# Fused tokenizer, attention and mixture-of-experts layer: weights of five groups in the rows, one class scatter, the seventh shared chunk behind the expert loop

## The chip, the cores and the metric

One core of one Trainium2 chip runs the whole layer in one launch. The metric is the device time in microseconds (us); lower is better. The engines are TensorE (PE), VectorE (DVE), ScalarE (ACT), GpSimd (POOL) and SyncE (SP). Each has an instruction queue of its own, and they meet in semaphores.

## The reference

For 16 images of 224 x 224 and 16 texts of 128 rows:

```
h = concat(class_token, patches(x) @ W.T + b) * pos      # 65 tokens per image
h = concat(h, txt)                                       # 193 tokens, 128 features
h = h + attention(layernorm(h))   # linear attention with rope, plus a 3-tap filter
x2 = layernorm(h)
shared = (silu(x2 @ sw1) * (x2 @ sw3)) @ sw2             # hidden size 256
scores = x2 @ gate_w.T            # 8 experts; the best 2 of scores + biases
p = sigmoid(two best scores); p = p / sum(p)
y_e = (silu(x2 @ w1[e]) * (x2 @ w3[e])) @ w2[e]
h = h + sum over the two experts of p * y_e + shared
```

## The kernel before, in words

There are 3088 tokens. Two images make a *group*, so there are G = 8 groups, 0 to 7; a group has three tiles of 128 tokens. The 16 class tokens are a 25th tile (`CLS`), handled with group 7. `hrow` holds all tokens as rows.

*Groups.* A loop takes the groups through tokenizing, attention, the second normalization (into `xd`), the gate's scores, the choice of experts (`choices`, line 1006) and the row numbers in the sorted buffer `xs_dram` (`place` on PE, then `places` and `positions` on DVE). Each token stands there twice, once for each of its experts. POOL writes the rows by indirect scatters (line 858), one for each tile and choice; the class tile takes two of 16 rows. So 50 scatters go out in the order of POOL's queue. Beside its features each row carries where its result belongs and a weight. For groups below `EARLIER` = 6, POOL works out both (`goals` and `shares`, lines 826 to 844, with one reciprocal on DVE and one exponential on ACT, `chances`), and `positions` waits for POOL there. For the later groups (tiles from `FROM` = 18) the rows carry weight 1, and the true weight is multiplied in at the end. The last groups are written out by hand on every engine (from lines 1185 on DVE and 1594 on PE).

*Shared FFN.* It goes in chunks of 384 tokens, 0 to 7, and chunk 8 with the class tokens. For each chunk and each half m of the hidden size: `shared_up` (two pairs of products on PE, lines 1574 and 1577), `shared_silu` on ACT (line 676), `shared_mul` on DVE (line 1159); then `shared_down` (PE, line 1589) and `shared_add` (DVE, line 1165). Chunks 0 to 6 have their ups and products ahead of the expert loop, between the last groups' work; chunk 6's down products, and chunks 7 and 8, stand behind it.

*Expert loop.* SP writes padding rows behind each expert's rows (line 411), waits for all scatters and gathers 128-row tiles from `xs_dram` (lines 418 and 435). For 56 tiles PE transposes (line 1660), multiplies by the two up matrices (line 1671, in three terms, for which `round_w13` on ACT and `remainder_w13` on DVE, line 1174, split the weights ahead), transposes (line 1680) and multiplies down (line 1691). DVE and ACT work between. POOL scatters each result to `y_dram` by token and choice (line 869).

*Tail.* SP gathers `y_dram` back in five chunks of tiles (0 to 5, 6 to 11, 12 to 17, 18 to 23, and 24), first for choice k = 0, then for k = 1 (line 445). DVE adds them to `hrow` by `add_results(c, k)`: plain chunks by one addition (line 1339), tiles that still need a weight by one weighted addition each (line 1333). For chunk 3 and k = 1, ACT multiplies the weights in beforehand (`late_results`, line 783). Each finished chunk goes out from SP and ACT (lines 452 and 795). The order of DVE's tail, from line 1342, is written out by hand.

Of the kernel before, what the change touches and what calls it, by code (L numbers as in the profile page):

```python
# [35 lines left out]
EARLIER = G - 2  # L36
# [68 lines left out]
def build(nc, patches, txt, w_tok, cls, pos, wqk, bqk, small, gate_b,  # L105
# [4 lines left out]
    with ctx:  # L110
# [128 lines left out]
        FINISHED = (0, 1, 3, 2, 4)  # L239
# [54 lines left out]
        def tiles_of(g):  # L294

            return list(range(3 * g, 3 * g + 3)) + ([CLS] if g == G - 1 else [])

        def rows_of(j):
            return B if j == CLS else P
# [13 lines left out]
        def up_banks(c, m):  # L313

            return [(5, 7), (2, 1), (4, 0)][(2 * c + m + (2 if c > EARLY else 0)) % 3]
# [38 lines left out]
        def _(sp):  # L354
# [53 lines left out]
            sp.dma_start(xs_dram[E * CAP:, :], pad).then_inc(padded, 16)  # L408
            sp.wait_ge(ends_done, 1)
# [6 lines left out]
            sp.wait_ge(scattered, 16 * 2 * J)  # L416
# [22 lines left out]
            for k in range(2):  # L439
                for u in range(U):  # L440
                    sp.wait_ge(y_sent[u], needed[k][u])
                for c in ((0, 1, 2, 3, 4), (0, 3, 4, 1, 2))[k]:
                    a, b = CHUNKS[c]
                    rows = rows_of(a)
                    sp.dma_start(y_rows[0:rows, k, a:b, :],
                                 y_dram[k * NID + a * P:k * NID + a * P + rows * (b - a), :].rearrange(
                                     "(j q) d -> q j d", q=rows)).then_inc(y_loaded[k][c], 16)
# [10 lines left out]
        def _(act):  # L458
# [231 lines left out]
            chances(G - 3)  # L690
# [20 lines left out]
            for rows, at in last_tiles:  # L711
                last = A(rs2[0:rows, at], lv2[0:rows, at], ACT.Exp, scale=-0.5)
            last.then_inc(rs2_done, 1)
            act.preload_act_table(ACT.Silu)
            shared_silu(1, 0)
            shared_silu(1, 1)
            shared_silu(2, 0)
            round_w13(4)
            act.wait_ge(nm2_done, G)
            A(xd[:, CLS - 1, 0, 0:D], hrow[:, CLS - 1, :], ACT.Identity, bias=nm2[:, CLS - 1:CLS],  # L720
              scale=rs2[:, CLS - 1:CLS]).then_inc(x2_done, 1)
            shared_silu(2, 1)
            act.wait_ge(x2_turned, G)
            nc.scalar.copy(x2T[:, 3 * P * (G - 1):3 * P * (G - 1) + 3 * P + B], bank[6][:, 0:3 * P + B]).then_inc(x2T_done, 1)
            round_w13(5)
# [4 lines left out]
            for j in tiles_of(G - 1):  # L730
                rows = rows_of(j)
                nc.scalar.copy(xd[0:rows, j, 1, 0:D], xd[0:rows, j, 0, 0:D]).then_inc(twice_done, 1)
            round_w13(6)
            shared_silu(3, 0)
# [6 lines left out]
            shared_silu(EARLY, 0)  # L741
            shared_silu(EARLY, 1)
# [36 lines left out]
            def late_results():  # L779

                act.wait_ge(y_loaded[1][len(CHUNKS) - 2], 16)
                for j in range(FROM, CLS):
                    last = A(y_rows[:, 1, j, :], y_rows[:, 1, j, :], ACT.Copy, scale=weight[:, 1, j - FROM:j - FROM + 1])
                last.then_inc(scaled, 1)

            act.wait_ge(weight_done, 1)
            shared_silu(EARLY + 1, 0)
# [10 lines left out]
        def _(pool):  # L798
# [47 lines left out]
            for g in range(G):  # L846
                if g < EARLIER:
                    goals(g)
                    shares(g)

                pool.wait_ge(pos_done, g + 1 + min(g + 1, EARLIER))
                pool.wait_ge(x2_done, g + 2 if g == G - 1 else g + 1)
                if g == G - 1:
                    pool.wait_ge(twice_done, len(tiles_of(g)))
                for j in tiles_of(g):
                    rows = rows_of(j)
                    for k in range(2):
                        nc.gpsimd.indirect_dma_start(  # L858
                            out=xs_dram[:, :], out_offset=bass.IndirectOffsetOnAxis(ap=pos_i[0:rows, j, k:k + 1], axis=0),
                            in_=xd[0:rows, j, k, :], in_offset=None).then_inc(scattered, 16)  # L860
# [14 lines left out]
        def _(dve):  # L875
# [316 lines left out]
            tap_behind(G - 1)  # L1192
            remainder_w13(0)
            places(G - 3)
# [3 lines left out]
            positions(G - 3)  # L1198
            remainder_w13(2)
# [9 lines left out]
            shared_add(0)  # L1209
            shared_mul(1, 0)  # L1210
# [5 lines left out]
            shared_mul(1, 1)  # L1216
# [3 lines left out]
            for j in (CLS - 3, CLS - 2, CLS):  # L1220
# [3 lines left out]
            last.then_inc(x2_done, 1)  # L1224
            remainder_w13(3)
            shared_mul(2, 0)
            shared_mul(2, 1)
            remainder_w13(4)
            shared_add(1)
# [4 lines left out]
            shared_add(2)  # L1234
            shared_mul(3, 0)
            shared_mul(3, 1)
            remainder_w13(5)
            then(V.tensor_scalar(ti[:, 0, :], bank[6][:, TOTAL_AT:TOTAL_AT + E], float(P - 1), None, ALU.add))
            then(V.tensor_scalar(ti[:, 1, :], ti[:, 0, :], 7, None, ALU.arith_shift_right))
            then(V.tensor_copy(tf[:], ti[:, 1, :]))  # L1240
            shared_mul(4, 0)
# [10 lines left out]
            V.tensor_scalar(t_w[:], tf[:], float(-P), float(CAP), ALU.mult, ALU.add)  # L1252
            then(V.tensor_tensor_scan(te[:], cst[:, C_ONES:C_ONES + E], tf[:], 0.0, ALU.mult, ALU.add))
            tile_no, tile_row = cst[:, C_TILE:C_TILE + 1], cst[:, C_TILE + 1:C_TILE + 2]
            V.tensor_scalar(gone[:, 1, :], te[:], tile_no, None, ALU.is_le)
            then(V.scalar_tensor_tensor(out=gone[:, 0, :], in0=te[:], scalar=tile_no, in1=t_w[:], op0=ALU.is_le, op1=ALU.mult))
            then(V.tensor_reduce(gone_sum[:], gone[:], AX.X, ALU.add))
            V.tensor_scalar(tab_cols[:, 0:1], gone_sum[:, 0:1], tile_row, float(E * CAP), ALU.add, ALU.min)
            V.tensor_scalar(tab_cols[:, 1:2], gone_sum[:, 1:2], float(E - 1), float(2 * D), ALU.min, ALU.mult
                            ).then_inc(cols_done, 1)  # L1260
# [3 lines left out]
            dve.wait_ge(cols_turned, 1)  # L1264
            V.tensor_copy(tab[:], bank[6][0:1, 0:2 * TILES].rearrange("p (k t) -> p k t", k=2)).then_inc(tab_done, 1)
            shared_mul(5, 1)
            remainder_w13(7)
            shared_mul(EARLY, 0)
            shared_mul(EARLY, 1)
# [54 lines left out]
            def add_results(c, k):  # L1324
# [6 lines left out]
                if a == CLS or (b == CLS and k == 0):  # L1331
                    for j in range(a, b):
# [10 lines left out]
            dve.wait_ge(sh_add, EARLY)  # L1343
            add_results(0, 0)
# [11 lines left out]
            add_results(1, 1)  # L1356
# [3 lines left out]
            add_results(2, 1)  # L1360
# [5 lines left out]
        def _(pe):  # L1366
# [236 lines left out]
            place(G - 3)  # L1603
            turn_queries(G - 1)
            mixed_rows(G - 2)
            pe.wait_ge(s_wexp, 96)
            shared_up(0, 0)
# [3 lines left out]
            shared_up(0, 1)  # L1611
# [7 lines left out]
            shared_down(0)  # L1619
            shared_up(2, 0)  # L1620
            place(G - 2)
            shared_up(2, 1)
            shared_down(1)
            turn_second(G - 1)
            gate(G - 1)
            shared_down(2)
            shared_up(3, 0)
            place(G - 1)
            shared_up(3, 1)
            shared_up(4, 0)  # L1630
            shared_down(3)
            shared_up(4, 1)
            shared_up(5, 0)
            shared_down(4)
# [4 lines left out]
            last.then_inc(cols_turned, 1)  # L1639
            shared_up(5, 1)  # L1640
            shared_up(EARLY, 0)
            shared_up(EARLY, 1)
            shared_down(EARLY - 1)
            pe.wait_ge(sh_mul, 2 * EARLY + 2)
# [63 lines left out]
            shared_up(EARLY + 1, 0)  # L1708
            for k in range(SLOTS):
                pe.wait_ge(ys_done[k], TILES // SLOTS)  # L1710
            shared_down(EARLY)
# [44 lines left out]
```

## Time and profile before

| What | Value |
|---|---|
| Time, median of 3 runs | 246.42 us (245.82 to 248.81) |
| The profiled execution: time, span | 246.49 us, 244.3 us |
| Busy share of the span: PE, DVE, ACT, POOL | 90%, 76%, 65%, 52% |
| The chain that ended last: PE, DVE, POOL | 49%, 22%, 7% |
| Moved by DMA | 31.77 MB, 130 GB/s in the mean |

The span runs from the first to the last instruction; the time also holds what lies around it, 2.19 us here. Busy shares are means over stages with different limits. The chain is followed back from the last instruction to what released it.

### The profile page before, as it was taken

How to read it: one execution, taken by the hardware profiler on the slowest of the kernel's cores; microseconds unless marked ns; L12 is line 12 of the kernel's file. 1: busy time of each engine (PE TensorE's matmuls, PEld its weight loads, DVE VectorE, ACT ScalarE, POOL GpSimd, SP SyncE). 2: the span in 40 equal slices, each digit the busy share in tenths (PEclk: the TensorE clock that was granted, in tenths of full speed). 3: DMA queues.
4: the chain of work that ended last, by engine and by line, in shares of the span. 5: the costliest groups of instructions: out<-in, count | busy, mean ns of one | idle time of the engine just before them, and what ended most of it. 6: DMA issues, size and time to landing. Idle time of an engine off the chain costs nothing.

```text
span 244.3 us, 5608 instructions
## 1 busy us (share of the span) xinstructions
PE 220.6 (90%) x1485; PEld 188.6 (77%) x1485; DVE 186.6 (76%) x717; ACT 158.0 (65%) x429; POOL 126.6 (52%) x165
## 2 busy tenths in 40 slices
PE   2798898989999999968989979999999999999970
PEld 2777787979898989856576657888888888888760
DVE  2457799999999999987987868666666666666784
ACT  3054786687777778869763165777777777777540
POOL 1310000205878686867777721666666666666720
PEclk9999999999999999999999999999999999999998
DMA  6999984050707010001112412414223332328397
GB/s 183 352 342 360 335 275 183 0 197 26 241 22 251 27 48 33 33 29 40 44 45 78 123 37 54 123 51 125 83 80 91 90 91 83 93 86 235 106 294 215
DMA packets 31565, 31.77 MB, mean 130 GB/s; under 512 B 4338, under 2 KB 27419, under 8 KB 30768
## 3 DMA queue, kind: packets, MB, share of 16 engines
q1 hardware_dynamic: 26824, 24.43, 33.3%
q0 software_dynamic: 3392, 6.38, 7.9%
q10 hardware_dynamic: 1320, 0.61, 0.9%
q8 instruction: 13, 0.21, 0.4%
q14 instruction: 16, 0.13, 0.2%
HBM read 22.85 MB, written 9.06 MB: 131 GB/s over the span
## 4 chain that ended last, share of the span: by engine, by line
PE 49%; DVE 22%; POOL 7%; issue 6%; ACT 5%; DMA 4%; SPq 3%; DVEq 0%; POOLq 0%; ACTq 0%
PE bank L1671 16%; PE bank L1691 10%; POOL xs_dram L858 6%; PE bank L1680 5%; DVE st L887 3%; DVE att L953 3%; PE bank L1660 3%; DVE att L944 3%; DMA xp_both<-in_patches 2%; PE bank L1383 2%; DVE att L946 2%; PE bank L1452 2%; PE bank L1466 2%; PE bank L1486 2%; DVE hrow L1339 2%
## 5 line engine op out<-in xcount | busy, mean ns | idle before, releaser
L869 POOL DMA_INDIRECT y_dram<-att,goal x56 | 55.8, 996 | 35.8 <-ACT att L767 35.2
L858 POOL DMA_INDIRECT xs_dram<-xd,pos_i x50 | 54.8, 1096 | 16.7 <-issue 13.1
L1383 PE MATMUL bank<-wt,xp_both 128*128 128x128 f32 x288 | 40.3, 294 | 6.5 <-DMA xp_both<-in_patches 6.5
L1383 PEld LDWEIGHTS bank<-wt,xp_both 128*128 128x128 f32 x288 | 38.0, 206 | 7.9 <-DMA xp_both<-in_patches 6.3
L1299 DVE CAST xsT_h<-bank 128x128 fp32r<-128x128 f32 x56 | 16.3, 292 | 24.1 <-PE bank L1660 23.4
L1691 PE MATMUL bank<-w_sb,att 128*128 x224 | 34.6, 277 | 0.0
L753 ACT ACTIVATE att<-bank 128x256 f32<-128x256 f32 x56 | 21.5, 384 | 19.0 <-PE bank L1671 19.0
L1691 PEld LDWEIGHTS bank<-w_sb,att 128*128 128x128 f32 x224 | 29.4, 191 | 0.4 <-issue 0.2
L1671 PE MATMUL bank<-xp_both,xsT_h 128*128 x56 | 26.8, 478 | 0.0
L1312 DVE TENSOR_TENSOR att<-att,bank 128x256 f32<-128x256 f32 x56 | 23.1, 413 | 1.6 <-ACT att L753 1.6
L767 ACT ACTIVATE att<-bank,goal 128x128 f32<-128x128 f32 x56 | 20.6, 368 | 4.7 <-PE bank L1691 0.7
L1671 PE MATMUL bank<-xp_both,xsT_l 128*128 x56 | 22.1, 395 | 0.0
L1680 PE MATMUL bank<-cst,att 128*128 128x128 f32 x112 | 21.5, 274 | 0.5 <-DVE att L1312 0.5
L1671 PE MATMUL bank<-w,xsT_h 128*128 x56 | 21.9, 392 | 0.0
L760 ACT COPY att<-bank 128x256 f32<-128x256 f32 x56 | 20.9, 372 | 0.8 <-PE bank L1680 0.8
L1680 PEld LDWEIGHTS bank<-cst,att 128*128 128x128 f32 x112 | 13.8, 140 | 5.8 <-DVE att L1312 1.5
L1301 DVE TENSOR_TENSOR xsT_l<-bank,xsT_h 128x128 fp32r<-128x128 f32 x56 | 16.3, 291 | 1.9
L676 ACT ACTIVATE sh_s<-bank 128x384 f32<-128x384 f32 (+1 forms) x18 | 8.0, 457 | 14.9 <-PE bank L1577 14.0
L1660 PE MATMUL bank<-cst,xs_all 128*128 128x128 f32 x56 | 15.3, 274 | 1.3 <-DMA xs_all<-xs_dram 1.3
L1308 DVE COPY goal<-xs_all 128x2 f32<-128x2 f32 x56 | 15.0, 267 | 0.0
L1574 PE MATMUL bank<-x2T,sw 128*128 128x384 f32 (+1 forms) x36 | 14.0, 469 | 0.5 <-DVE sh_h L1159 0.4
L556 ACT ACTIVATE xrow<-hrow,nm,rs 128x128 f32<-128x128 f32 x24 | 10.9, 486 | 4.7 <-DVE nm L906 2.9
(223 smaller groups left out, 501.0 us busy)
## 6 DMA issues: line engine op xcount, KB each, us to landing
xp_both<-in_patches SPq DMA_DIRECT2D x6, 1152.0 KB, 5.3
xs_all<-xs_dram SPq DMA_DIRECT2D x56, 65.0 KB, 1.8
xd<-y_dram SPq DMA_DIRECT2D x8, 384.0 KB, 4.9
w<-in_w SPq DMA_DIRECT2D x2, 1024.0 KB, 10.2
y_dram<-att,goal POOLq DMA_INDIRECT x56, 2.3
xs_dram<-xd,pos_i POOLq DMA_INDIRECT x50
xp_both<-in_patches SPq DMA_DIRECT2D x1, 768.0 KB, 5.7
hrow<-in_txt SPq DMA_DIRECT2D x2, 384.0 KB, 7.9
```

Of the source, the lines that this page charges most:

```text
L753: A(hs[q][:], bank[2 + q][:, 0:HID], ACT.Silu).then_inc(silu_done[at], 1)
L760: nc.scalar.copy(hmT[q][:], bank[4 + q][:, 0:HID].rearrange("p (m t) -> p m t", m=2)).then_inc(hmT_done[at], 1)
L767: A(ys[buf][:], bank[6 + q][:, 0:D], ACT.Copy, scale=goal[buf][:, 1:2]).then_inc(ys_done[at], 1)
L858: nc.gpsimd.indirect_dma_start(out=xs_dram[:, :], out_offset=bass.IndirectOffsetOnAxis(ap=pos_i[0:rows, j, k:k + 1], axis=0), in_=xd[0:row ...
L869: nc.gpsimd.indirect_dma_start(out=y_dram[:, :], out_offset=bass.IndirectOffsetOnAxis(ap=goal[u][:, 0:1].bitcast(I32), axis=0), in_=ys[u][ ...
L1299: V.tensor_copy(xsT_h[q][:], bank[q][:, 0:P]).then_inc(xh_done, 1)
L1312: V.tensor_tensor(hm[q][:], hs[q][:], bank[2 + q][:, HID:2 * HID], ALU.mult).then_inc(hm_done[at], 1)
L1383: M(ps[:, 0:D], xp[p][:, k, :], wt[:, k, :], start=(k == 0), stop=False)
L1660: T(bank[q][:, 0:P], xs[u][:, 0:D], ident).then_inc(tx_done[slot(u, 0)], 1)
L1671: last = M(bank[2 + q][:, 0:2 * HID], x[q][:], w[:, bass.ds(first * 2, 2 * HID)], start=(i == 0), stop=(i == 2))
L1680: last = T(bank[4 + q][:, P * m:P * m + P], hm[q][:, P * m:P * m + P], ident)
L1691: last = M(bank[6 + q][:, 0:D], hmT[q][:, m, :], w[:, bass.ds(first + m * D, D)], start=(m == 0), stop=(m == 1))
```

## The change

`EARLIER` becomes 5, so `FROM` becomes 15: group 5's rows carry weight 1, and its three tiles are weighted in the tail, within chunk 2. The class tile's two scatters become one of 32 rows: two small copies on SP bring the second choice's rows and row numbers behind the first's, and POOL waits for both before that scatter. On DVE, ACT and PE the last groups' normalization, choices and row numbers move ahead of shared products and weight splits, and the table of the expert tiles moves ahead of chunk 3's products. Chunk 6's up products, activations and products move behind the expert loop on all three engines; on DVE its products stand ahead of the first result addition. The order in which chunks are finished changes with it. The diff, cut:

```diff
-EARLIER = G - 2
+EARLIER = G - 3
 FROM = 3 * EARLIER
 LATE = J - FROM
...
-FINISHED = (0, 1, 3, 2, 4)
+FINISHED = (0, 2, 3, 1, 4)
...
-    return [(5, 7), (2, 1), (4, 0)][(2 * c + m + (2 if c > EARLY else 0)) % 3]
+    return [(5, 7), (2, 1), (4, 0)][(2 * c + m + (2 if c >= EARLY else 0)) % 3]
...
     sp.dma_start(xs_dram[E * CAP:, :], pad).then_inc(padded, 16)
+    sp.wait_ge(twice_done, len(tiles_of(G - 1)))
+    sp.dma_start(xd[B:2 * B, CLS, 0, :], xd[0:B, CLS, 1, :]).then_inc(s_cls, 16)
+    sp.wait_ge(pos_done, G + EARLIER)
+    sp.dma_start(pos_i[B:2 * B, CLS, 0:1], pos_i[0:B, CLS, 1:2]).then_inc(s_cls, 16)
     sp.wait_ge(ends_done, 1)
...
-    sp.wait_ge(scattered, 16 * 2 * J)
+    sp.wait_ge(scattered, 16 * (2 * J - 1))
...
-        for c in ((0, 1, 2, 3, 4), (0, 3, 4, 1, 2))[k]:
+        for c in ((0, 1, 2, 3, 4), (0, 3, 4, 2, 1))[k]:
...
     rstd2(G - 2)
-    chances(G - 3)
     key_sums(G - 1)
     norm2(G - 2)
...
     act.preload_act_table(ACT.Silu)
+    act.wait_ge(nm2_done, G)
+    A(xd[:, CLS - 1, 0, 0:D], hrow[:, CLS - 1, :], ACT.Identity, bias=nm2[:, CLS - 1:CLS],
+      scale=rs2[:, CLS - 1:CLS]).then_inc(x2_done, 1)
     shared_silu(1, 0)
     shared_silu(1, 1)
     shared_silu(2, 0)
-    round_w13(4)
-    act.wait_ge(nm2_done, G)
-    A(xd[:, CLS - 1, 0, 0:D], hrow[:, CLS - 1, :], ACT.Identity, bias=nm2[:, CLS - 1:CLS],
-      scale=rs2[:, CLS - 1:CLS]).then_inc(x2_done, 1)
-    shared_silu(2, 1)
     act.wait_ge(x2_turned, G)
     nc.scalar.copy(x2T[:, 3 * P * (G - 1):3 * P * (G - 1) + 3 * P + B], bank[6][:, 0:3 * P + B]).then_inc(x2T_done, 1)
-    round_w13(5)
+    round_w13(4)
...
     for j in tiles_of(G - 1):
         rows = rows_of(j)
         nc.scalar.copy(xd[0:rows, j, 1, 0:D], xd[0:rows, j, 0, 0:D]).then_inc(twice_done, 1)
+    shared_silu(2, 1)
+    round_w13(5)
+    shared_silu(3, 0)
     round_w13(6)
-    shared_silu(3, 0)
     shared_silu(3, 1)
     round_w13(7)
     shared_silu(4, 0)
     shared_silu(4, 1)
     shared_silu(5, 0)
     shared_silu(5, 1)
-    shared_silu(EARLY, 0)
-    shared_silu(EARLY, 1)
...
         act.wait_ge(y_loaded[1][len(CHUNKS) - 2], 16)
-        for j in range(FROM, CLS):
+        for j in range(CHUNKS[-2][0], CLS):
             last = A(y_rows[:, 1, j, :], y_rows[:, 1, j, :], ACT.Copy, scale=weight[:, 1, j - FROM:j - FROM + 1])
...
     act.wait_ge(weight_done, 1)
+    shared_silu(EARLY, 0)
+    shared_silu(EARLY, 1)
     shared_silu(EARLY + 1, 0)
...
@@ -853,8 +856,10 @@
         if g == G - 1:
             pool.wait_ge(twice_done, len(tiles_of(g)))
         for j in tiles_of(g):
-            rows = rows_of(j)
-            for k in range(2):
+            rows = 2 * B if j == CLS else P
+            if j == CLS:
+                pool.wait_ge(s_cls, 64)
+            for k in range(1 if j == CLS else 2):
                 nc.gpsimd.indirect_dma_start(
                     out=xs_dram[:, :], out_offset=bass.IndirectOffsetOnAxis(ap=pos_i[0:rows, j, k:k + 1], axis=0),
                     in_=xd[0:rows, j, k, :], in_offset=None).then_inc(scattered, 16)
...
     tap_behind(G - 1)
+    places(G - 3)
+    positions(G - 3)
     remainder_w13(0)
-    places(G - 3)
     remainder_w13(1)
     attended(G - 1)
     mixed(G - 1)
-    positions(G - 3)
-    remainder_w13(2)
     second_rows(G - 1)
...
     choices(G - 2)
-    shared_add(0)
-    shared_mul(1, 0)
     dve.wait_ge(rs2_done, G)
     dve.wait_ge(st2_done, G + 1)
...
     last.then_inc(nm2_done, 1)
-    shared_mul(1, 1)
     places(G - 2)
     positions(G - 2)
...
     last.then_inc(x2_done, 1)
+    shared_mul(1, 0)
+    shared_add(0)
+    shared_mul(1, 1)
+    remainder_w13(2)
     remainder_w13(3)
-    shared_mul(2, 0)
-    shared_mul(2, 1)
-    remainder_w13(4)
-    shared_add(1)
     choices(G - 1)
     places(G - 1)
     positions(G - 1)
...
-    shared_add(2)
-    shared_mul(3, 0)
-    shared_mul(3, 1)
-    remainder_w13(5)
+    shared_mul(2, 0)
+    shared_add(1)
+    shared_mul(2, 1)
     then(V.tensor_scalar(ti[:, 0, :], bank[6][:, TOTAL_AT:TOTAL_AT + E], float(P - 1), None, ALU.add))
...
+    V.tensor_scalar(t_w[:], tf[:], float(-P), float(CAP), ALU.mult, ALU.add)
...
+    V.tensor_scalar(tab_cols[:, 1:2], gone_sum[:, 1:2], float(E - 1), float(2 * D), ALU.min, ALU.mult
+                    ).then_inc(cols_done, 1)
+    shared_mul(3, 0)
+    shared_add(2)
+    shared_mul(3, 1)
+    remainder_w13(4)
+    dve.wait_ge(cols_turned, 1)
+    V.tensor_copy(tab[:], bank[6][0:1, 0:2 * TILES].rearrange("p (k t) -> p k t", k=2)).then_inc(tab_done, 1)
+    remainder_w13(5)
     shared_mul(4, 0)
     shared_add(3)
...
     shared_mul(4, 1)
-    V.tensor_scalar(t_w[:], tf[:], float(-P), float(CAP), ALU.mult, ALU.add)
...
-    V.tensor_scalar(tab_cols[:, 1:2], gone_sum[:, 1:2], float(E - 1), float(2 * D), ALU.min, ALU.mult
-                    ).then_inc(cols_done, 1)
     remainder_w13(6)
     shared_add(4)
     shared_mul(5, 0)
-    dve.wait_ge(cols_turned, 1)
-    V.tensor_copy(tab[:], bank[6][0:1, 0:2 * TILES].rearrange("p (k t) -> p k t", k=2)).then_inc(tab_done, 1)
     shared_mul(5, 1)
     remainder_w13(7)
-    shared_mul(EARLY, 0)
-    shared_mul(EARLY, 1)
...
+        if a == CLS or (b == CLS and k == 0) or a < FROM < b:
+            if a < FROM:
+                V.tensor_tensor(hrow[:, a:FROM, :], hrow[:, a:FROM, :], y_rows[:, k, a:FROM, :], ALU.add)
+            for j in range(max(a, FROM), b):
                 last = V.scalar_tensor_tensor(
                     out=hrow[0:rows, j, :], in0=y_rows[0:rows, k, j, :], scalar=weight[0:rows, k, j - FROM:j - FROM + 1],
                     in1=hrow[0:rows, j, :], op0=ALU.mult, op1=ALU.add)
...
     dve.wait_ge(weight_done, 1)
     dve.wait_ge(sh_add, EARLY)
+    shared_mul(EARLY, 0)
+    shared_mul(EARLY, 1)
     add_results(0, 0)
     add_results(1, 0)
...
     shared_mul(EARLY + 2, 1)
-    add_results(1, 1)
+    add_results(2, 1)
     shared_add(EARLY + 1)
     dve.wait_ge(sh_add, EARLY + 2)
     add_results(3, 1)
-    add_results(2, 1)
+    add_results(1, 1)
     shared_add(EARLY + 2)
...
     place(G - 3)
+    pe.wait_ge(s_wexp, 96)
+    shared_up(0, 0)
     turn_queries(G - 1)
     mixed_rows(G - 2)
-    pe.wait_ge(s_wexp, 96)
-    shared_up(0, 0)
+    shared_up(0, 1)
     pe.wait_ge(rr_done, G)
     turn_turned(G - 1)
     sums(G - 1)
-    shared_up(0, 1)
     attend(G - 1)
...
     shared_up(1, 1)
     shared_down(0)
+    place(G - 2)
     shared_up(2, 0)
-    place(G - 2)
+    turn_second(G - 1)
+    gate(G - 1)
     shared_up(2, 1)
     shared_down(1)
-    turn_second(G - 1)
-    gate(G - 1)
+    place(G - 1)
+    shared_up(3, 0)
+    shared_up(3, 1)
     shared_down(2)
-    shared_up(3, 0)
-    place(G - 1)
-    shared_up(3, 1)
     shared_up(4, 0)
-    shared_down(3)
-    shared_up(4, 1)
-    shared_up(5, 0)
-    shared_down(4)
     pe.wait_ge(cols_done, 1)
...
     last.then_inc(cols_turned, 1)
+    shared_down(3)
+    shared_up(4, 1)
+    shared_up(5, 0)
+    shared_down(4)
     shared_up(5, 1)
-    shared_up(EARLY, 0)
-    shared_up(EARLY, 1)
     shared_down(EARLY - 1)
-    pe.wait_ge(sh_mul, 2 * EARLY + 2)
+    pe.wait_ge(sh_mul, 2 * EARLY)
     pe.wait_ge(tab_done, 1)
...
     expert_steps(pe, pe_step, 4)
-    shared_up(EARLY + 1, 0)
+    shared_up(EARLY, 0)
     for k in range(SLOTS):
         pe.wait_ge(ys_done[k], TILES // SLOTS)
+    shared_up(EARLY, 1)
+    shared_up(EARLY + 1, 0)
     shared_down(EARLY)
     shared_up(EARLY + 1, 1)
     shared_up(EARLY + 2, 0)
```

## Rows read from the trace of the kernel before

**Rows 1.** Page, part 1: busy us and share of the span, by engine.

```profile
PE 220.6 (90%) x1485; PEld 188.6 (77%) x1485; DVE 186.6 (76%) x717; ACT 158.0 (65%) x429; POOL 126.6 (52%) x165
```

**Rows 2.** Page, part 4: the chain that ended last, by engine.

```profile
PE 49%; DVE 22%; POOL 7%; issue 6%; ACT 5%; DMA 4%; SPq 3%; DVEq 0%; POOLq 0%; ACTq 0%
```

**Rows 3.** Timeline, POOL: start us, us, engine line op; first and last of many.

```profile
112.13 0.96 POOL L858 DMA_INDIRECT xs_dram<-xd,pos_i  x1 [0.30 <-issue]
...
116.45 1.10 POOL L858 DMA_INDIRECT xs_dram<-xd,pos_i  x1 [0.29 <-POOL xd L843]
...
141.21 0.85 POOL L858 DMA_INDIRECT xs_dram<-xd,pos_i  x1 [0.30 <-issue]
```

**Rows 4.** The chain in order of time, 97 to 147: start us, us, what.

```profile
143.18 0.02 SPq L416
```

**Rows 5.** Timeline, DVE, 110 to 147.

```profile
110.98 0.60 DVE L977 SCALAR_TENSOR_TENSOR hl<-xT,cols,hl 128x384 f32<-128x384 f32 x1
...
116.02 0.55 DVE L995 TENSOR_TENSOR hrow<-bank,hrow 128x384 f32<-128x384 f32 x1
...
120.51 0.21 DVE L1031 TENSOR_REDUCE bc<-bc 128x8 bf16<-128x32 bf16 x1
...
123.93 0.67 DVE L1174 TENSOR_TENSOR w<-w,xp_both 128x512 fp32r<-128x512 f32 x1
...
127.33 0.19 DVE L1011 TENSOR_TENSOR scb<-sc,gateb_sb 128x32 f32<-128x32 f32 x1
...
130.93 0.15 DVE L1057 TENSOR_REDUCE pos_i<-pos 128x4 int32<-128x8 f32 x1
...
143.84 0.55 DVE L1159 TENSOR_TENSOR xrow<-sh_s,bank 128x384 f32<-128x384 f32 x1 [0.73 <-ACT sh_s L676]
```

**Rows 6.** Timeline, PE, 104 to 147.

```profile
105.30 0.30 PE L1426 MATMUL bank<-cst,att 128*128 128x128 f32 x1 [1.49 <-DVE att L930]
...
115.03 0.40 PE L1416 MATMUL bank<-cst,s_all 128*128 128x128 f32 x2
...
137.38 1.58 PE L1589 MATMUL bank<-sw_sb,sh_h 128*128 128x128 f32 x12 [0.26 <-DVE sh_h L1159]
...
138.79 0.55 PE L1637 MATMUL bank<-cst,tab_cols 128*128 128x56 f32 x4
...
140.53 0.81 PE L1574 MATMUL bank<-x2T,sw 128*128 128x384 f32 x2
...
141.82 0.81 PE L1574 MATMUL bank<-x2T,sw 128*128 128x384 f32 x2
...
145.36 0.33 PE L1660 MATMUL bank<-cst,xs_all 128*128 128x128 f32 x1 [0.74 <-DMA xs_all<-xs_dram]
...
146.48 0.49 PE L1671 MATMUL bank<-xp_both,xsT_h 128*128 x1
```

**Rows 7.** Timeline, all engines, 228 to the end.

```profile
228.85 2.69 DVE L1339 TENSOR_TENSOR hrow<-hrow,xd 128x768 f32<-128x768 f32 x3
...
230.51 0.81 PE L1574 MATMUL bank<-x2T,sw 128*128 128x384 f32 x2
...
231.45 1.91 DVE L1333 SCALAR_TENSOR_TENSOR hrow<-xd,weight,hrow 128x128 f32<-128x128 f32 x7
...
233.29 0.53 DVE L1159 TENSOR_TENSOR sh_h<-sh_s,bank 128x384 f32<-128x384 f32 x1
...
237.06 0.96 DVE L1339 TENSOR_TENSOR hrow<-hrow,xd 128x768 f32<-128x768 f32 x1 [0.87 <-DMA xd<-y_dram]
...
240.57 0.34 DVE L1333 SCALAR_TENSOR_TENSOR hrow<-xd,weight,hrow 16x128 f32<-16x128 f32 x1
```

**Rows 8.** DMA issues: count, KB each, median us to landing.

```profile
cls_in<-in_pos ACTq DMA_DIRECT2D x1, 8.0 KB, 3.0
...
w_sb<-in_w SPq DMA_DIRECT2D x1, 0.5 KB, 12.7
```

**Rows 9.** Windows, 230.5 to the end: busy us by engine, PEclk, DMA share, GB/s.

```profile
230.50:244.30 13.80, 7.08 (x46) 5.46 (x44) 9.25 (x21) 3.35 (x11) 2.60 (x3) 0.92 0.87 229
```

More of the change, by code:

```diff
@@ L1240, in _ @@
             then(V.tensor_copy(tf[:], ti[:, 1, :]))
+            V.tensor_scalar(t_w[:], tf[:], float(-P), float(CAP), ALU.mult, ALU.add)
+            then(V.tensor_tensor_scan(te[:], cst[:, C_ONES:C_ONES + E], tf[:], 0.0, ALU.mult, ALU.add))
+            tile_no, tile_row = cst[:, C_TILE:C_TILE + 1], cst[:, C_TILE + 1:C_TILE + 2]
+            V.tensor_scalar(gone[:, 1, :], te[:], tile_no, None, ALU.is_le)
+            then(V.scalar_tensor_tensor(out=gone[:, 0, :], in0=te[:], scalar=tile_no, in1=t_w[:], op0=ALU.is_le, op1=ALU.mult))
+            then(V.tensor_reduce(gone_sum[:], gone[:], AX.X, ALU.add))
+            V.tensor_scalar(tab_cols[:, 0:1], gone_sum[:, 0:1], tile_row, float(E * CAP), ALU.add, ALU.min)
+            V.tensor_scalar(tab_cols[:, 1:2], gone_sum[:, 1:2], float(E - 1), float(2 * D), ALU.min, ALU.mult
[7 more added lines that the diff above has]
+            remainder_w13(5)
             shared_mul(4, 0)
@@ L1251, in _ @@
             shared_mul(4, 1)
-            V.tensor_scalar(t_w[:], tf[:], float(-P), float(CAP), ALU.mult, ALU.add)
[L1253 to L1258, printed above, removed]
-            V.tensor_scalar(tab_cols[:, 1:2], gone_sum[:, 1:2], float(E - 1), float(2 * D), ALU.min, ALU.mult
-                            ).then_inc(cols_done, 1)
             remainder_w13(6)
@@ L1330, in add_results @@
                     dve.wait_ge(fin_first, len(CHUNKS))
-                if a == CLS or (b == CLS and k == 0):
-                    for j in range(a, b):
+                if a == CLS or (b == CLS and k == 0) or a < FROM < b:
+                    if a < FROM:
+                        V.tensor_tensor(hrow[:, a:FROM, :], hrow[:, a:FROM, :], y_rows[:, k, a:FROM, :], ALU.add)
+                    for j in range(max(a, FROM), b):
                         last = V.scalar_tensor_tensor(
```

## The prediction

> **What bounds the kernel now.** I read the page's shares of busy time first, then its chain of waits, then the timelines of POOL, DVE and PE around the chain's turns. By busy time TensorE leads, 90% against VectorE's 76% [rows 1], but the chain that ended last holds only 49% PE and 22% DVE [rows 2], so the binding engine changes from stage to stage. All times below are microseconds from the span's start. Two stages matter.
>
> The first is the **head of the expert loop**. POOL sends row scatters in its queue's order: 20 of them (6, 6 and 8 for groups 5, 6 and 7) from 116.45 to 141.21, one each 1.30 [rows 3]. The last lands and releases SP's gathers at 143.18 [rows 4]; the first gathered tile is transposed at 145.36, and the first expert product starts at 146.48 [rows 6]. Just before that, PE runs the shared FFN's chunks without a pause worth naming, so two queues arrive at the loop almost together.
>
> The second is the **tail**. DVE ends its loop work and starts adding first-choice results at 228.85, while PE is still in its last tiles: the product behind the loop starts at 230.51. From 228.85 to its last addition (240.57 plus 0.34) DVE is idle only 0.87 in one piece, for a transfer [rows 7]. So in the tail DVE's queue is the path, then the last output transfers (240.91 to the span's end, 244.3).
>
> **The change, part by part.**
>
> *Weights of five groups in the rows.* Group 5's goals and shares leave POOL. Its queue was free for the next scatter at 113.39 (112.13, plus 0.96, plus the usual 0.30) and began group 5 at 116.45 [rows 3]: 3.06 come out, if group 5's row numbers are ready. They are: `places` and `positions` now stand before the weight splits and no longer wait for POOL, so they end near 112.1 (estimate: 0.6 behind the tap that started at 110.98 and let the next operation go at 111.5 [rows 5]). The price is in the tail (below), and one ACT exponential less.
>
> *Row numbers ahead of shared products.* On DVE, `second_rows(7)` began at 116.02 [rows 5] behind a split and the wait for POOL. Now it waits only for the transposes that start at 115.03 [rows 6]; these last 0.40, with a little for the semaphore 0.44 (estimate), so 115.47, 0.55 earlier. All up to the end of group 6's choices (120.51 plus 0.21) moves along: 120.17. Numbers of group 6 follow at once on PE and DVE, estimate 1.1, near 121.3. Between group 6's choices and group 7's lay 6.6 (120.72 to 127.33 [rows 5]); three shared operations of 0.55 leave this stretch, with their stalls some 2.0 (estimate), while one split of 0.67 only replaces another. So group 7's choices start near 120.17 + 4.6 = 124.8, and its numbers, 3.75 behind as before (127.33 to 130.93 plus 0.15), are ready at 128.5 instead of 131.1.
>
> *One class scatter.* POOL: group 5 from 113.39, six of them at 1.26 to 1.30 to 121.1; group 6 from about 121.6; group 7 from 129.3 (its numbers wait less than POOL's backlog), and the seventh and last scatter from 137.0 instead of 141.21. Landing takes what it took (143.18 less 141.21), so the gathers are released at 139.0, 4.2 earlier. What is added: two small copies in SP's queue, one behind `twice_done`, one behind the last numbers, each landing on the semaphore that POOL awaits before the class scatter. SP only waited there; what is queued behind them, the padding rows and then the gathers, is pushed by two issues of about 0.55, covered by the 139.0 they wait for anyway. How long the copies take the trace doesn't show. From below: a 16-row load of 8 KB landed in 3.0; from above, the slowest landing of that view, 12.7 [rows 8]. I take 3.0, the nearer in shape: issued at about 128.8, landed by 132, five ahead of need. With 12.7 the class scatter would start at 141.5: no scatter gained.
>
> *PE's order.* `shared_up(0, 0)` moves into the 1.49 in which PE waited ahead of `turn_queries` (105.30 [rows 6]); an up product pair takes 1.29 (140.53 to 141.82), so it costs nothing; if that cover is gone, 1.29 at most would go onto the path. ACT's reordered work lies in its waits for PE's products. The seventh chunk's two pairs (2.58) leave PE's queue ahead of the loop. Behind group 7's `place` (near 127.2) PE still has six pairs (7.74), four downs at 1.41 (137.38 to 138.79; 5.64), the table's transposes and the place (at most 0.75): 141.3. Before the last down it now waits for chunk 5's product, which no other pair covers any more: a pair starting at 141.82 had its product at 143.84 plus 0.55, so 1.28 behind the pair's end [rows 5, 6]. With 0.2 of small stalls PE is ready for the loop at **142.8**, later than the first gathered rows (139.0 plus the 2.18 from 143.18 to 145.36: 141.2). Before the first expert product DVE still adds chunk 5: 1.3 from transposition to product in place of 1.12, 144.1 against 146.48. **Head: −2.4.** Here PE, not POOL, ends last.
>
> *The seventh chunk behind the last tile.* Its pairs take the place of those that started at 230.51 and run to 233.1 in the old clock of the loop's end. Its two products are put **first** in DVE's tail queue, ahead of `add_results(0, 0)`. The second pair starts at 230.51 + 1.29 = 231.80; its product is done 2.57 later (141.82 to 144.39 [rows 5, 6]), at 234.37. So DVE, free at 228.85, stands until 234.37 with all five first-choice additions queued behind a product that they don't need: **+5.5**. Everything after them in DVE's queue, the ACT scaling and the outputs wait in turn.
>
> *Weights of group 5 in the tail.* Chunk 2 (tiles 12 to 17) is now added half plainly, half tile by tile, for both choices: three weighted tiles at 0.263 (231.45 to 233.29 for seven [rows 7]) and half of 0.87 (three additions from 228.85 to 231.45): 1.2 instead of 0.87, twice: +0.7. ACT scales six tiles as before. Against this the 0.87 in which DVE waited for a transfer goes, since the data is there by then. Tail: 5.5 + 0.7 − 0.9 = **+5.3**.
>
> **Sum.** The loop itself (56 tiles) is unchanged. 5.3 − 2.4 = +2.9 on the profiled execution's 246.49 (span 244.3): 249.4. The median of the runs shown is 246.42, so the same number stands for it.
>
> **A rule against this.** The rows show DVE without slack in the tail and TensorE waiting there [rows 7]. The Trainium skill, Perfetto Trace Analysis, section Identifying the Most-Contended Engine, says that the engine with the highest occupancy is to be optimized first; by that, TensorE's shorter head would decide and the sum would be 246.49 − 2.4 = 244.1, the number of rival 1. The chain of waits speaks against it here, with DVE's queue holding the end [rows 2, 7]; the same page's next section grants that regimes change.
>
> **Rivals.**
>
> 1. *Not slower: DVE's stand is hidden, because the tail belongs to the transfers.* DMA engines are 0.87 busy from 230.5 on, at 229 GB/s [rows 9]. Were the second-choice gathers and the outputs the limit, DVE's 5.5 would vanish in them and only the head's 2.4 would show: 244.1. For it: that share. Against: DVE waited once, 0.87, for a transfer.
> 2. *The class copies bind.* Place: POOL's wait before the last scatter. It decides once the copies land later than 138.6 (POOL's 137.0 plus the 1.6 by which PE is later than the gathers), 9.8 after issue. At 12.7 the gathers come at 143.5, the head gains nothing, and 5.3 stays: 251.8.
> 3. *PE's last wait is shorter, or the head is bound by POOL alone.* Then 4.2 comes off: 247.6.
> 4. *Row numbers don't come earlier* (the stretch between the choices keeps its length because transposition, copy and scores set it): only the dropped scatter counts, −1.3: 250.5.
>
> **Chances.** The forecast 0.60, rival 1 0.13, rival 2 0.07, rival 3 0.10, rival 4 0.10. Two per cent, about what a measurement of this kernel can tell from no change, is 4.9: below 241.5 is faster, above 251.3 slower. Faster needs rival 1 with a head of twice my size: 0.03. Slower is rival 2 and the forecast's upper edge (DVE's wait above 7): 0.10. Within: 0.87. The range takes the forecast with rivals 3 and 4 and half of rival 2: 246.5 to 251.6; rival 1 is left out.
>
> **What would show it.** First scatter of group 5 near 113.4, last scatter near 137, gathers released near 139, the first expert product near 144.1 with PE's last shared down just before it. In the tail: a hole of more than 5 on DVE between its last loop product and the seventh chunk's products, first-choice additions only after them, and no wait for a transfer later. Wrong would be: additions that start as soon as the loop ends, outputs that end as early as now, or POOL waiting before its last scatter.

## The result, and the profile after

After: 251.75 us, median of 4 runs (250.97 to 253.44); before, 246.95 (4 runs, 245.82 to 248.81). The ratio is 1.022, interval 1.018 to 1.026. The ratio counts fast executions alone: without the run of 248.81 the median before is 246.42, and the difference 5.3 instead of the 4.8 between the two medians. The forecast was 249.4, 2.9 more than before, with a range of 246.5 to 251.6: the direction was right, the loss was larger, and the time lies a little outside the range. The prediction had put 0.87 on staying within two per cent; the interval lies across that line. The profiled execution took 252.06, its span 250.2 against 244.3, so the traces have 5.9 to account for.

The page of the changed kernel, busy shares and the chain by engine, answering to [rows 1, 2]:

```profile
PE 222.2 (89%) x1477; PEld 189.1 (76%) x1485; DVE 188.1 (75%) x724; ACT 157.7 (63%) x428; POOL 122.5 (49%) x157
...
PE 57%; DVE 27%; ACT 5%; issue 4%; SPq 3%; DMA 3%; DVEq 0%; ACTq 0%
```

POOL has left the chain (7% before), DVE's share rose from 22 to 27%. I take the head first, then the tail. POOL's timeline in the changed kernel (start us, us, engine line op): first scatters of groups 5, 6 and 7, and the last of all, against [rows 3].

```profile
113.75 0.96 POOL L863 DMA_INDIRECT xs_dram<-xd,pos_i  x1 [0.30 <-issue]
...
121.89 0.96 POOL L863 DMA_INDIRECT xs_dram<-xd,pos_i  x1 [0.85 <-DVE pos_i L1062]
...
129.93 0.96 POOL L863 DMA_INDIRECT xs_dram<-xd,pos_i  x1 [0.30 <-issue]
...
137.62 0.88 POOL L863 DMA_INDIRECT xs_dram<-xd,pos_i  x1 [0.31 <-issue]
```

The queue runs 3.6 ahead of before (137.62 against 141.21), and the last scatter, which must wait for the two class copies, stood only the usual 0.31. PE's timeline up to the loop, against [rows 6]:

```profile
127.62 0.19 PE L1502 MATMUL bank<-bc,tri_b 128*128 128x32 bf16 x1
...
127.81 0.89 PE L1581 MATMUL bank<-x2T,sw 128*128 128x384 f32 x2
...
129.31 0.91 PE L1581 MATMUL bank<-x2T,sw 128*128 128x384 f32 x2
...
138.44 1.58 PE L1596 MATMUL bank<-sw_sb,sh_h 128*128 128x128 f32 x12 [0.34 <-DVE sh_h L1164]
...
142.57 1.58 PE L1596 MATMUL bank<-sw_sb,sh_h 128*128 128x128 f32 x12 [1.26 <-DVE sh_h L1164]
144.01 0.41 PE L1665 MATMUL bank<-cst,xs_all 128*128 128x128 f32 x2
145.40 0.50 PE L1676 MATMUL bank<-xp_both,xsT_h 128*128 x1 [0.98 <-DVE xsT_l L1304]
```

The first transposition of the loop (144.01) has no wait for a transfer any more: PE's own queue, with the wait of 1.26 for chunk 5's product, sets the start of the loop. The first expert product starts 1.08 earlier than before (145.40 against 146.48). Tail of the changed kernel, all engines, against [rows 7]:

```profile
227.83 0.42 DVE L1315 TENSOR_TENSOR att<-att,bank 128x256 f32<-128x256 f32 x1 [0.93 <-ACT att L754]
...
232.00 0.55 DVE L1164 TENSOR_TENSOR xrow<-sh_s,bank 128x384 f32<-128x384 f32 x1 [3.74 <-ACT sh_s L680]
...
233.14 0.55 DVE L1164 TENSOR_TENSOR xrow<-sh_s,bank 128x384 f32<-128x384 f32 x1 [0.59 <-ACT sh_s L680]
...
233.61 1.82 DVE L1344 TENSOR_TENSOR hrow<-hrow,xd 128x768 f32<-128x768 f32 x2
...
239.03 0.40 PE L1581 MATMUL bank<-x2T,sw 128*128 128x16 f32 x2 [1.98 <-DVE sh_h L1164]
...
240.92 2.90 PE L1596 MATMUL bank<-sw_sb,sh_h 128*128 128x128 f32 x12 [1.16 <-DVE xrow L1164]
...
243.86 0.56 DVE L1170 TENSOR_TENSOR hrow<-bank,hrow 128x384 f32<-128x384 f32 x1 [1.35 <-PE bank L1596]
...
246.50 0.34 DVE L1338 SCALAR_TENSOR_TENSOR hrow<-xd,weight,hrow 16x128 f32<-16x128 f32 x1
```

Two more rows of the kernel before, for comparison: DVE's last loop product and PE's down products of chunk 7.

```profile
228.51 0.42 DVE L1312 TENSOR_TENSOR att<-att,bank 128x256 f32<-128x256 f32 x1 [0.93 <-ACT att L753]
...
235.85 1.58 PE L1589 MATMUL bank<-sw_sb,sh_h 128*128 128x128 f32 x12 [0.46 <-DVE xrow L1159]
```

DVE stands 3.74 and 0.59 ahead of chunk 6's two products, and the first addition starts at 233.61 instead of 228.85. Later PE waits 1.98 and 1.16 for DVE, and chunk 7's down products take 2.90, where before they took 1.58. The windows of the changed kernel say why (window and its length in us, busy us of PE, PEld, DVE, ACT and POOL, then the granted clock as a share of full speed, DMA share, GB/s):

```profile
238.00:239.00 1.00, 0.00 (x0) 0.00 (x0) 1.00 (x4) 0.00 (x0) 0.00 (x0) 1.00 0.00 0
239.00:240.00 1.00, 0.73 (x4) 0.62 (x4) 1.00 (x2) 0.18 (x1) 0.00 (x0) 0.70 0.00 0
240.00:241.00 1.00, 0.08 (x1) 0.11 (x1) 0.85 (x3) 0.13 (x2) 0.00 (x0) 0.50 0.00 0
```

PE is nearly idle from 237, the granted clock falls from 1.00 to 0.50, which is the 1.2 GHz level, and it is at that level when the 12 products of 240.92 start. The Trainium skill (TensorE: Matmul & The Clock Gate, What's actually happening) says that the gate follows how busy PE has been lately; these rows agree with it. DMA is idle in these three microseconds too, so no transfer holds up this stretch.

**The account**, span against span. The loop (its first expert product) starts 1.08 earlier, but takes 0.40 longer (82.43 against 82.03, from the start of the first product on PE to the start of the last one on DVE). From there to the start of the first addition: 5.78 against 0.34, +5.44. From the first addition to the end of the last: 13.23 against 12.06, +1.17. The last transfers: 3.36 against 3.39. Together −1.08 + 0.40 + 5.44 + 1.17 − 0.03 = +5.9.

### The profile page after: what moved, and what is told of

Read it like the earlier page. It is cut to its first block, busy times and chain, and to the rows that moved or that the text cites. A ratio compares the mean times of both kernels' runs of the same rounds, so it can differ in the third digit from the quotient of the medians.

```text
span 250.2 us, 5598 instructions
## 1 busy us (share of the span) xinstructions
PE 222.2 (89%) x1477; PEld 189.1 (76%) x1485; DVE 188.1 (75%) x724; ACT 157.7 (63%) x428; POOL 122.5 (49%) x157
## 4 chain that ended last, share of the span: by engine, by line
PE 57%; DVE 27%; ACT 5%; issue 4%; SPq 3%; DMA 3%; DVEq 0%; ACTq 0%
PE bank L1676 15%; PE bank L1696 10%; PE bank L1685 5%; PE bank L1596 4%; DVE att L949 3%; DVE att L958 3%; DMA xp_both<-in_patches 3%; DVE st L892 3%; PE bank L1390 2%; PE bank L1665 2%; DVE att L951 2%; PE bank L1459 2%; PE bank L1581 2%; PE bank L1493 2%; PE bank L1584 2%
## 5 line engine op out<-in xcount | busy, mean ns | idle before, releaser
L874 POOL DMA_INDIRECT y_dram<-att,goal x56 | 55.0, 982 | 38.8 <-ACT att L768 38.5
L863 POOL DMA_INDIRECT xs_dram<-xd,pos_i x49 | 53.7, 1096 | 17.0 <-issue 12.8
L1390 PE MATMUL bank<-wt,xp_both 128*128 128x128 f32 x288 | 39.7, 290 | 7.6 <-DMA xp_both<-in_patches 7.6
L1390 PEld LDWEIGHTS bank<-wt,xp_both 128*128 128x128 f32 x288 | 37.4, 203 | 9.2 <-DMA xp_both<-in_patches 5.8
L1596 PEld LDWEIGHTS bank<-sw_sb,sh_h 128*128 128x128 f32 x84 | 11.3, 211 | 5.4 <-issue 4.2
```

Of the source, the lines that this page charges most:

```text
L863: nc.gpsimd.indirect_dma_start(out=xs_dram[:, :], out_offset=bass.IndirectOffsetOnAxis(ap=pos_i[0:rows, j, k:k + 1], axis=0), in_=xd[0:row ...
L874: nc.gpsimd.indirect_dma_start(out=y_dram[:, :], out_offset=bass.IndirectOffsetOnAxis(ap=goal[u][:, 0:1].bitcast(I32), axis=0), in_=ys[u][ ...
L1390: M(ps[:, 0:D], xp[p][:, k, :], wt[:, k, :], start=(k == 0), stop=False)
L1596: last = M(bank[3][0:rows, D * t:D * t + D], hidden_of(c, m)[:, P * t:P * t + rows], sw2_sb[:, m, :], start=(m == 0), stop=(m == 1))
```

## Experiments

In the expectations, theory A is that DVE stands at chunk 6's products with the additions queued behind them. Ratios are against the kernel before on the same chip (median 246.11 for products behind the additions, only chunk 6, all but chunk 6 and the first filler; 246.21 for the others).

**Products behind the additions.** The changed kernel, with one move on DVE:

```
-shared_mul(EARLY, 0)
-shared_mul(EARLY, 1)
 add_results(0, 0) ... add_results(4, 0)
+shared_mul(EARLY, 0)
+shared_mul(EARLY, 1)
```

> The changed kernel with one edit: on VectorE the two products of chunk 6 stand behind the five first-choice additions. Theory A (VectorE stands 5.4 us in its tail queue, and the late chain of products then leaves TensorE idle until its clock halves): VectorE's first addition starts within 0.5 us of its last loop product, the hole of 3.7 us goes, and so does the halved clock before chunk 7's down products; the end comes 4 to 6 us earlier, a time of 246 to 248 us. Theory B (the output transfers and group 5's weights set the tail): less than 1.5 us come back, 250 to 252 us. Theory C (the loss sits ahead of the loop): nothing, 251.7 us.

Measured: 247.23, ratio 1.0056 (1.0025 to 1.0087), span 245.3. DVE's timeline in this kernel:

```profile
226.86 0.42 DVE L1315 TENSOR_TENSOR att<-att,bank 128x256 f32<-128x256 f32 x1 [0.93 <-ACT att L754]
227.20 1.82 DVE L1344 TENSOR_TENSOR hrow<-hrow,xd 128x768 f32<-128x768 f32 x2
...
232.03 1.00 DVE L1164 TENSOR_TENSOR xrow<-sh_s,bank 128x384 f32<-128x384 f32 x2
...
234.85 0.56 DVE L1170 TENSOR_TENSOR hrow<-bank,hrow 128x384 f32<-128x384 f32 x1 [0.85 <-PE bank L1596]
...
241.56 0.34 DVE L1338 SCALAR_TENSOR_TENSOR hrow<-xd,weight,hrow 16x128 f32<-16x128 f32 x1
```

The additions follow the loop at once, the products find their data ready, and the ratio falls by 1.6 points, some 4 us. Theory A is shown. The 4 us hold the clock's part too, which this run by itself can't tell from the stand's. What is left of the change is still no gain: additions to end are 14.70 against 12.06, since chunk 6's two products (1.00), the weights of group 5 and stalls of 0.43, 0.85 and 0.32 now lie in the tail, while the wait of 0.87 for a transfer is gone.

**Only chunk 6 moved.** The kernel before, with chunk 6's pairs and SiLUs behind the loop and its products ahead of the additions, with the banks and wait counts that go with it, and nothing else. In short:

```
 PE:   -shared_up(EARLY, 0); shared_up(EARLY, 1)       (ahead of the loop)
       +shared_up(EARLY, 0); ...; shared_up(EARLY, 1)  (behind it)
 ACT:  shared_silu(EARLY, 0), (EARLY, 1) behind weight_done
 DVE:  +shared_mul(EARLY, 0); shared_mul(EARLY, 1)     (ahead of add_results(0, 0))
```

> The kernel before with one part of the change: chunk 6's up products, activations and products behind the expert loop, with VectorE's products ahead of the first-choice additions; scatters, weights and the order ahead of the loop as before. Theory A: the loop starts no earlier (the gathered rows bound it, first expert product 146.3 to 146.7 us), the tail grows by 5.4 plus 1.0 to 1.5 us: 253 to 254 us. Theory B: 247 to 249 us.

Measured: 252.93, just under the 253 to 254 expected, ratio 1.0296 (1.0266 to 1.0325). Timeline of this kernel's tail:

```profile
232.24 0.56 DVE L1159 TENSOR_TENSOR xrow<-sh_s,bank 128x384 f32<-128x384 f32 x1 [3.74 <-ACT sh_s L676]
...
233.86 2.69 DVE L1337 TENSOR_TENSOR hrow<-hrow,xd 128x768 f32<-128x768 f32 x3
...
240.78 2.90 PE L1589 MATMUL bank<-sw_sb,sh_h 128*128 128x128 f32 x12 [1.27 <-DVE xrow L1159]
```

The same stand of 3.74, the same 2.90 for the down products: this part alone makes the whole loss. The other three parts are not in it, so neither effect needs them.

**All but chunk 6.** The changed kernel with that part undone (the same lines, the other way round).

> The changed kernel with chunk 6 back ahead of the expert loop on TensorE, ScalarE and VectorE; everything else of the change stays. Theory A: TensorE's queue ahead of the loop grows by 2.6 us but covers the wait of 1.3 us for chunk 5's product, so the first expert product starts near 146.7 us; the tail is that of the kernel before plus 0.7 us for group 5's weights, less up to 0.9 us of a wait for a transfer: 246 to 247.5 us. Theory C: 250 us or more, since the loss would stay.

Measured: 247.36, ratio 1.0041 (1.0017 to 1.0064). The timeline of this kernel has no stand behind the loop:

```profile
147.34 0.50 PE L1678 MATMUL bank<-xp_both,xsT_h 128*128 x1 [0.74 <-DVE xsT_l L1306]
...
229.53 0.42 DVE L1317 TENSOR_TENSOR att<-att,bank 128x256 f32<-128x256 f32 x1 [0.93 <-ACT att L756]
229.87 1.82 DVE L1346 TENSOR_TENSOR hrow<-hrow,xd 128x768 f32<-128x768 f32 x2
...
242.00 0.34 DVE L1340 SCALAR_TENSOR_TENSOR hrow<-xd,weight,hrow 16x128 f32<-16x128 f32 x1
```

The loop starts late here (147.34, where 146.7 was expected) although the last scatter starts at 137.19: PE carries chunk 6's two pairs again, and in this execution its clock fell ahead of the loop, which costs some 1.5 by the rows of the last section (an estimate). How much of the lateness is the clock's stays open, though: this execution, at a mean granted clock of 0.989, took 247.54, and others of the same kernel at 0.993 to 0.995 took 246.07 to 247.36. From the first addition to the end of the last it is 12.47 against 12.06: the weights, less what is saved of the wait (0.58 of it is left here), cost 0.4. So the three other parts bring nothing by themselves; the interval even lies a little above 1.

**One class scatter alone.** The kernel before with the two copies and one scatter less:

```
+sp.dma_start(xd[B:2 * B, CLS, 0, :], xd[0:B, CLS, 1, :])
+sp.dma_start(pos_i[B:2 * B, CLS, 0:1], pos_i[0:B, CLS, 1:2])
-for k in range(2):
+for k in range(1 if j == CLS else 2):
```

> The kernel before with one part of the change: the class tile's rows in one scatter of 32, with the two small copies. POOL's last scatter starts 1.26 us earlier, without a wait in front of it if the copies land in 3 us; TensorE, whose shared work ends 0.7 us before the first gathered tile, then bounds the loop's start: 0.5 to 0.8 us faster, 245.3 to 245.6 us. If the copies bind (the rival of the prediction): POOL waits before its last scatter and the time is 246 us or more.

Measured: 246.27, ratio 0.9985 (0.9958 to 1.0011): no difference, a missed expectation (0.5 to 0.8 faster). Timeline of this kernel:

```profile
139.42 0.87 POOL L864 DMA_INDIRECT xs_dram<-xd,pos_i  x1 [0.30 <-issue]
...
144.58 0.55 DVE L1171 TENSOR_TENSOR hrow<-bank,hrow 128x384 f32<-128x384 f32 x1
144.64 0.41 PE L1666 MATMUL bank<-cst,xs_all 128*128 128x128 f32 x2 [0.65 <-DMA xs_all<-xs_dram]
...
145.79 0.50 PE L1677 MATMUL bank<-xp_both,xsT_h 128*128 x1 [0.75 <-DVE xsT_l L1307]
```

POOL does not wait for the copies and is one scatter shorter. To compare executions whose beginnings differ, I count from the first scatter of group 4: the first expert product comes 41.28 after it (145.79 less 104.51) against 41.37 before (146.48 less 105.11). The transposition still waits for its transfer, but the chain of waits no longer goes through it: DVE can split the transposed rows only behind chunk 5's addition of 144.58, which stands in its queue behind chunk 6's second product, and that waited for PE and ACT. Two queues that end together give back nothing when one of them is shortened.

**A busy TensorE.** To test the second effect, the changed kernel with products whose results nobody reads, 6 behind chunk 8's first pair of up products and 4 behind its second, ahead of chunk 7's down products (arguments cut):

```
 shared_up(EARLY + 2, 0)
+for _ in range(6): M(bank[6][:, 0:3 * P], sw13[:, 0:P], x2T[:, 0:3 * P])
 shared_up(EARLY + 2, 1)
+for _ in range(4): (the same)
 shared_down(EARLY + 1)
```

> The changed kernel with ten matmuls more behind the expert loop, six after chunk 8's first pair and four after its second, whose results nobody reads: they fill the stretch in which TensorE waits for VectorE. Theory A with the clock as its second part: the granted clock stays at 1.0 there, chunk 7's down products take 1.4 us in place of 2.9, and the time falls by 1.2 to 1.6 us, to about 250.3 us. If the clock has no part in the end: 251.7 us, or a little more for the added work.

Measured: 252.74, ratio 1.0273 (1.0245 to 1.0302), no gain. Timeline of this kernel:

```profile
236.60 4.12 PE L1722 MATMUL bank<-x2T,sw 128*128 128x384 f32 x12
...
240.92 2.83 PE L1725 MATMUL bank<-x2T,sw 128*128 128x384 f32 x8
...
243.58 1.50 PE L1596 MATMUL bank<-sw_sb,sh_h 128*128 128x128 f32 x12
```

The clock held, and the down products took 1.50. But each filler shows as two records and takes some 0.67 (an estimate: the last four hold PE from 240.92 to 243.58), so the filler itself delayed the down products from 240.92 to 243.58. The expected 250.3 was missed because the filler was too large, and the question was still open. Hence **half the filler** (3 and 2):

> The filler again, with half the matmuls (three after chunk 8's first pair, two after its second), since each of the ten lasted 0.65 us by the trace of that run and pushed chunk 7's down products back by some 2.5 us. If the halved clock costs time: the granted clock stays at 1.0, chunk 7's down products start within 0.4 us of where they started without filler and last 1.4 to 1.6 us, and the time falls by 1.0 to 1.5 us against the changed kernel, to 250.3 to 250.8 us or a ratio to the kernel before of about 1.015. If the clock has no part: the ratio stays at 1.02 or above.

Measured: 250.53, ratio 1.0147 (1.0103 to 1.0191). The window over this kernel's last additions, and its timeline:

```profile
237.00:246.00 9.00, 6.21 (x32) 3.89 (x31) 8.29 (x22) 2.45 (x9) 0.00 (x0) 1.00 0.40 112
```

```profile
233.71 1.82 DVE L1344 TENSOR_TENSOR hrow<-hrow,xd 128x768 f32<-128x768 f32 x2
...
241.02 1.58 PE L1596 MATMUL bank<-sw_sb,sh_h 128*128 128x128 f32 x12
...
242.63 0.56 DVE L1170 TENSOR_TENSOR hrow<-bank,hrow 128x384 f32<-128x384 f32 x1
245.28 0.34 DVE L1338 SCALAR_TENSOR_TENSOR hrow<-xd,weight,hrow 16x128 f32<-16x128 f32 x1
```

With the clock at 1.00 throughout, the down products take 1.58, DVE waits for nothing at 242.63, and from the first addition to the end of the last it is 11.91, against 13.23 in the changed kernel and 12.06 before. More work on TensorE makes this tail 1.3 shorter. That the clock is the second cause is shown; the totals' intervals overlap a little, so its size is taken from that stretch.

**Another order of the tail.** The first experiment, and on DVE `add_results(0, 1)` and chunk 7's two products ahead of `shared_add(6)`, on PE `shared_up(7, 1)` ahead of `shared_down(6)`, against the stalls of 0.43 and 0.85:

> The products of chunk 6 behind the five first-choice additions, and one step more: on VectorE the first second-choice addition and both products of chunk 7 ahead of chunk 6's shared addition, on TensorE chunk 7's second pair ahead of chunk 6's down products. The three stalls that VectorE still showed in the tail with the products behind the additions alone (0.43, 0.85 and 0.32 us) should go for the most part: 1.0 to 1.6 us less than that run's 247.2 us, so 245.6 to 246.3 us. If the outputs' transfers set the tail, nothing comes of it: 247.2 us.

Measured: 246.65, ratio 1.0009 (0.9987 to 1.0031), over the 245.6 to 246.3 expected. The tail itself came out as expected: from the first addition to the end of the last it is 13.70, 1.0 less than in the first experiment. The profiled execution, 247.49, is one in which the clock fell ahead of the loop (last section).

**And chunk 5's wait.** On top of that, chunk 5's hidden values go into another buffer, so that its pair no longer stands behind chunk 4's down products:

```
-if c in (EARLY, EARLY + 2) else sh_h[m]
+if c in (EARLY - 1, EARLY, EARLY + 2) else sh_h[m]
 PE:  shared_up(5, 1) ahead of shared_down(4)
 DVE: shared_mul(5, 0), shared_mul(5, 1) ahead of shared_add(4)
```

> The kernel with the tail's order mended, and ahead of the loop chunk 5's hidden values in the buffer that chunk 6 also uses, so that chunk 5's second pair can stand ahead of chunk 4's down products. If TensorE's wait of 1.26 us for chunk 5's product is what starts the loop 1.0 to 1.3 us later than forecast: that wait falls to 0.7 us or less, the first expert product starts 1.0 to 1.3 us sooner after group 7's place, and the time is 1.0 to 1.3 us below that of the kernel with the tail's order alone, near 244.7 us. If the gathered rows bound the loop's start: no change, 245.9 us.

Measured: 244.81, ratio 0.9947 (0.9923 to 0.9971), the only version here whose interval lies below the kernel before, though by no more than half a per cent. It is 1.8 under the last experiment, where 1.0 to 1.3 were expected. Timeline of this kernel:

```profile
140.97 1.61 PE L1596 MATMUL bank<-sw_sb,xrow 128*128 128x128 f32 x12 [0.65 <-DVE hrow L1170]
...
143.84 0.50 PE L1676 MATMUL bank<-xp_both,xsT_h 128*128 x1 [0.92 <-DVE xsT_l L1304]
...
226.04 1.82 DVE L1344 TENSOR_TENSOR hrow<-hrow,xd 128x768 f32<-128x768 f32 x2
...
239.40 0.34 DVE L1338 SCALAR_TENSOR_TENSOR hrow<-xd,weight,hrow 16x128 f32<-16x128 f32 x1
```

PE's last wait is 0.65 instead of 1.26, and counted from the first scatter of group 4 the loop starts after 38.79 (143.84 less 105.05), against 39.94 in the changed kernel (145.40 less 105.46). These 1.15 are gain in the head that the old order with its uncovered wait had held back.

## Where the prediction was right, and where it was wrong

- **The seventh chunk's stand** (forecast +5.5): +5.44, right in place, cause and size. Without it the additions follow the loop at once (products behind the additions); with it alone the whole loss is there (only chunk 6 moved). So rival 1, a stand hidden by transfers (244.1), fell. With it fell what the prediction had worked out by the rule of the most-contended engine in the Trainium skill (Perfetto Trace Analysis, Identifying the Most-Contended Engine): TensorE, the busiest engine before with 90%, was relieved ahead of the loop, and the time rose by 2.2%.
- **The rest of the tail** (forecast weights +0.7, wait −0.9, together −0.2): +1.17. This is the step that failed. Together the two terms hold: with the clock held the stretch measured 11.91, which is 0.15 less than before. What is missing is a term. I followed DVE's queue and let PE keep its old durations; but with DVE 4.8 later, PE waits for DVE's products between small pieces of work, and its clock fell to the lower level just before chunk 7's down products. They took 2.90 instead of 1.58, and DVE, which had not waited for them before, waited 1.35.
- **The head** (forecast −2.4): −1.08 at the first expert product. The order of arrivals was right: scatters, 137.62 against a forecast of 137.0, were ahead of PE, and PE bound the loop; SP's gathers went out at 140.31 (143.41 before), later than the forecast 139.0, but still ahead of PE. What was mis-sized, the second step that failed, is PE's stretch from `place` to the first transposition: 16.39 against 15.6. The first two pairs behind `place` took 1.50 and 1.40 and not 1.29 (+0.32); two pairs that end in a wait count by their own end, 1.45 to that wait (+0.32, twice 0.16); the small wait was 0.34 and not 0.2. The wait for chunk 5's product was forecast at 1.28 and came at 1.26. Of the other 0.5 or so, 0.35 lay already in this execution's first scatter of group 4 (105.46 against 105.11).
- **The loop, taken as unchanged**: 0.40 longer in this profile. The other profiles have 81.84 to 82.22 for the same stretch; what set it here was not settled.
- **Class copies** (rival 2, 251.8): its time lies near the measured one, but its mechanism did not occur; POOL stood 0.31 before the last scatter, the usual pause between two scatters. Rival 3 (POOL alone binds, 247.6) fell by PE's rows at 142.57 and 144.01. Rival 4 fell too: group 5's scatters started at 113.75, forecast 113.4, and group 7's at 129.93, forecast 129.3.
- **The dropped scatter** lay in the head's sum without a price of its own. Alone it is worth nothing, because the shared work of PE, ACT and DVE reaches the loop at the same time as POOL's queue.

The sum with the measured terms, 5.44 + 1.17 − 1.08 + 0.40, is 5.9, against 5.3 − 2.4 = 2.9: the tail cost 1.3 more than forecast (13.23 less 11.91, the clock's part, is all of it), the head gained 1.3 less, and the loop took 0.4 more. All three misses go the same way, so no luck hides in the sum.

## What to carry to other kernels

Work moved out of an engine's busy stretch must not be put at the front of another engine's in-order queue where its inputs are late: put behind work that is ready, the same two products cost 4 us less. When a change makes one engine late, go through the durations of those that wait for it again as well: here a TensorE that had paused came back at half its clock, and twelve products took 2.90 instead of 1.58. And before a queue is shortened, see how far behind it the next one arrives, since only that distance can be won.

## What the runs showed of the hardware

TensorE's clock also fell in a place where the change has no pause of its own. Timeline and windows of the kernel with another order of the tail, ahead of the loop:

```profile
123.05 0.97 PE L1493 MATMUL bank<-cols,x2T 128*128 128x8 f32 x8 [0.72 <-ACT x2T L725]
123.95 1.35 PE L1581 MATMUL bank<-x2T,sw 128*128 128x384 f32 x2
```

```profile
124.00:125.00 1.00, 1.00 (x3) 0.59 (x3) 0.77 (x7) 0.94 (x6) 0.99 (x1) 0.64 0.02 4
125.00:126.00 1.00, 1.00 (x3) 0.60 (x2) 0.93 (x10) 0.08 (x1) 0.70 (x1) 0.50 0.20 67
```

The experiment with the products behind the additions runs the same instructions here with the same idle pieces (0.48, 0.19 and 0.72), and there the clock stayed at 1.00 from 120 to 130; its first expert product came 39.94 behind the first scatter of group 4 (144.67 less 104.73), here 41.45 (146.06 less 104.61). So the same order of work costs 1.5 more in one execution than in another. The times of this kernel divide in the same way: six executions with a mean granted clock of 0.993 to 0.998 took 245.60 to 246.38, five at 0.988 to 0.989 took 246.92 to 247.56. A fall ahead of the loop is in the profiles of five kernels of this study, one of them that of chunk 6 alone, whose head has the old order; so it does not need the change. Whether the new order makes it more frequent, and why one execution has it and another has not, stays open.
